# The denominators of a rational convolution: transformed, inverted and scaled in earlier stages

## The reference

```python
a = concat([ones, denumerator])          # 9 taps for each of 64 x 64 channel pairs
b = concat([zeros, numerators])
H_trunc = rfft(b, n=Lx) / rfft(a, n=Lx)  # Lx = 256
H_tf = h0 + rfft(irfft(H_trunc, n=Lx), n=2 * Lx)[0]
Y = einsum('bli,ijl->blj', rfft(x, n=2 * Lx), H_tf)
y = irfft(Y)[..., :Lx, :]
```

## Time and profile before

| | |
|---|---|
| three timed runs | 837.86, 838.05, 841.0 us (median 838.05) |
| the profiled execution | 834.53 us, of which the span of the profile is 832.7 |
| PE busy | 632.0 us (76%) |
| DVE busy | 520.1 us (62%) |
| ACT busy | 330.3 us (40%) |
| POOL busy | 272.7 us (33%) |
| granted TensorE clock, mean | 0.855 of full speed |

### The profile page before, as it was taken

How to read it: one execution, slowest core, us unless ns; L and a number is a source line. 1 busy time by engine, 2 the same in 40 slices (tenths; PEclk the granted TensorE clock), 3 DMA queues, 4 the chain that set the end, 5 groups by cost and what they waited for, 6 DMA issues and landing times. The chain is left out here.

```text
span 832.7 us, 13076 instructions
## 1 busy us (share of the span) xinstructions
PE 632.0 (76%) x4688; PEld 424.1 (51%) x4688; DVE 520.1 (62%) x1402; ACT 330.3 (40%) x634; POOL 272.7 (33%) x233
## 2 busy tenths in 40 slices
PE   3894573776887479999899999977878573998864
PEld 2673462654775342322577878862222122984753
DVE  1242977752655746667457885537466897833897
ACT  1231120443554224455236553223424974931552
POOL 6714701513200101001167674512010798400420
PEclk9995886797999559899899997977888765999987
DMA  7854410100000000000100000040001000000011
GB/s 217 270 176 113 119 39 0 67 3 0 1 1 0 28 41 1 0 2 1 35 6 12 14 7 13 2 179 1 0 1 35 0 1 0 2 3 0 1 26 25
DMA packets 18784, 30.05 MB, mean 36 GB/s; under 512 B 6434, under 2 KB 15650, under 8 KB 18082
## 3 DMA queue, kind: packets, MB, share of 16 engines
q1 hardware_dynamic: 16162, 19.80, 7.8%
q0 software_dynamic: 2560, 9.44, 3.7%
HBM read 27.25 MB, written 1.05 MB: 34 GB/s over the span
## 5 line engine op out<-in xcount | busy, mean ns | idle before, releaser
L166 POOL TENSOR_TENSOR norm_rstd<-norm_var,minus_half 128x16 f32<-128x16 f32 x16 | 46.9, 2929 | 307.8 <-DVE norm_var L160 307.8
L1267 ACT ACTIVATE m_g<-PS,w_slot 128x512 f32<-128x512 f32 x96 | 60.8, 685 | 72.4 <-PE PS L1321 65.0
L1220 DVE TENSOR_TENSOR m_gw<-m_g,PS 128x512 f32<-128x512 f32 x96 | 61.3, 683 | 39.5 <-PE PS L1329 27.3
L1321 PE MATMUL PS<-m_xT,w_slot 64*128 64x512 f32 x192 | 71.7, 698 | 7.0 <-ACT m_g L1267 6.8
L1345 PE MATMUL PS<-m_gw,w_slot 128*64 128x512 f32 x192 | 57.2, 666 | 0.0
L106 PE MATMUL PS<-w_base 128*128 128x128 f32 x316 | 47.4, 307 | 12.5 <-PEq L2647 11.2
L106 PEld LDWEIGHTS PS<-w_base 128*128 128x128 f32 x316 | 41.5, 159 | 15.8 <-issue 13.5
L2066 ACT COPY rat_xf<-PS 64x512 f32<-64x512 f32 x32 | 33.0, 1032 | 9.9 <-PE PS L2122 9.7
L1329 PE MATMUL PS<-m_gT,m_sel 48*128 48x512 bf16 x96 | 24.3, 421 | 15.5 <-DVE m_gw L1220 9.8
L148 DVE BATCH_NORM_STATS2 norm_halves<-H 128x6 f32<-128x64 f32 x256 | 33.8, 209 | 1.2 <-PEq L2647 1.2
L2122 PE MATMUL PS<-w_slot,norm_xn 128*128 128x512 f32 x32 | 24.4, 906 | 13.2 <-DVE norm_xn L2003 13.2
(11 more groups left out here) (339 smaller groups left out, 1634.1 us busy)
## 6 DMA issues: line engine op xcount, KB each, us to landing
rff_routed<-in_routed SPq DMA_DIRECT2D x64, 129.0 KB, 2.1
rat_hf<-in_rat_taps SPq DMA_DIRECT2D x1, 2048.0 KB, 7.8
w_slot<-in_w_rat SPq DMA_DIRECT2D x1, 1589.0 KB, 11.2
w_slot<-in_w_win SPq DMA_DIRECT2D x1, 1378.5 KB, 5.8
w_slot<-in_w_m SPq DMA_DIRECT2D x1, 1329.0 KB, 5.6
w_slot<-in_w_early SPq DMA_DIRECT2D x1, 1092.0 KB, 8.7
out<-H SPq DMA_DIRECT2D x8, 128.0 KB, 2.2
win_v<-win_v SPq DMA_DIRECT2D x8, 97.5 KB, 2.1
```

What stands on the lines that cost most here:

```text
L166: nc.gpsimd.tensor_tensor(N.rstd[:], N.var[:], C.minus_half[:], ALU.pow).then_inc(S["norm_rstd"], 1)
L1220: nc.vector.tensor_tensor(gw[:, i % 2, half, :], g[:, i % 2, half, :], gate_bank[half], ALU.mult)\
L1267: nc.scalar.activation(g[:, i % 2, half, :], hid_bank[(n - 1) % 3], ACT.Gelu, bias=b1[:, s:s + 1])\
L1321: nc.tensor.matmul(hid_bank[n % 3], w1[lane(half), s, :], pair_of(xT, pair)[lane(half)], start=True, stop=True).then_inc(S["hid_ps"], 1)
```

## The change

The numerators' part stays in the rational stage; the denominators' part is distributed over four stages before it. New class `Denominators`:

- `transform(s)` on PE: two matmuls of 32 rows for step s. Steps 0 and 1 stand behind the last chunk of the attention and ahead of batch norm's sums, 2 and 3 behind the sums, 4 and 5 at the end of the stage, 6 and 7 in m1 behind the logits. The transposed results of batch norm use three banks of PSUM in turn, not four.
- `move(s)` on ACT: a copy and a square. Steps 0 to 2 ahead of the rectifiers, 3 to 5 behind them, 6 and 7 in m1 ahead of the exponential, there as four instructions of 128x512 each.
- `add_squares(s)` on DVE: steps 0 to 5 in m1 ahead of the gates, 6 and 7 behind the split. POOL did this before.
- `invert` on DVE: 32 pieces of 128x128 in place of 8 instructions of 128x512: 20 in m1, 8 at the end of win, 4 at the start of m2.
- `scale(s)` on DVE: the denominator times the inverse, 128x1024, 7 between m2's steps and the last behind them. POOL's multiplication of `ht` (L1939) goes.

In the rational stage DVE keeps the products and the norm, POOL keeps an add and a subtract a step, ACT keeps the copies of the token spectra. The taps are loaded in two halves (the denominators' at the start of batch norm's stage), and the small computation at the last frequency (`at_nyquist`) moves from the start to behind the sixth products.

```diff
@@ batchnorm_attention, ACT
             staircase(act, stages, 7)
+            for s in range(SQUARED_FIRST):
+                C.denominators.move(act, s, [PS[2 + s % 2][:]])
             for c in range(CHUNKS):
                 act.wait_ge(S["centred"], c + 1)
                 nc.scalar.activation(junk[:, at], FT[:, at], ACT.Relu, ...).then_inc(S["y"], 1)
+            for s in range(SQUARED_FIRST, SQUARED_TAIL):
+                C.denominators.move(act, s, [PS[2 + s % 2][:]])
@@ batchnorm_attention, PE
+            pe.wait_ge(S["FT"], CHUNKS)
+            denominators(0)
+            denominators(1)
             pe.wait_ge(S["lower_sum"], CHUNKS + 1)
...
+            denominators(2)
+            denominators(3)
             for c in range(CHUNKS):
                 pe.wait_ge(S["y"], c + 1)
-                if c >= W:
-                    pe.wait_ge(S["h_new"], c - W + 1)
+                if c >= 3:
+                    pe.wait_ge(S["h_new"], c - 2)
...
+            for s in range(4, SQUARED_TAIL):
+                denominators(s)
@@ gelu_moe, DVE
+            if again:
+                for s in range(SQUARED_TAIL):
+                    C.denominators.add_squares(v, s)
+            else:
+                for n in range(4 * STEPS - 4, 4 * STEPS - 2):
+                    C.denominators.invert(v, n)
             gate_logits(0)
...
             split_gates(0)
+            if again:
+                for s in range(SQUARED_TAIL, STEPS):
+                    C.denominators.add_squares(v, s)
...
+                if again and i in M1_PIECES:
+                    C.denominators.invert(v, M1_PIECES.index(i))
+                if not again and i in M2_PIECES:
+                    C.denominators.invert(v, 4 * STEPS - 2 + M2_PIECES.index(i))
+                if not again and i in M2_SCALES:
+                    C.denominators.scale(v, M2_SCALES.index(i))
...
+            if not again:
+                C.denominators.scale(v, STEPS - 1)
             add_output(NP - 1)
@@ gelu_moe, ACT: ahead of exponentials(0)
+                for s in range(SQUARED_TAIL, STEPS):
+                    C.denominators.move(act, s, spare_banks[s % 2])
@@ gelu_moe, PE: between logits(0) and hidden(0)
+                for s in range(SQUARED_TAIL, STEPS):
+                    C.denominators.transform(pe, C, s, spare_banks[s % 2])
@@ window_attention, DVE
+                if n in WIN_PIECES:
+                    C.denominators.invert(vec, len(M1_PIECES) + WIN_PIECES.index(n))
@@ new
+SQUARED_FIRST = 3
+SQUARED_TAIL = 6
+M1_PIECES = (1, 3, 4, 5, 6, 7, 8, 9, 13, 16, 17, 19, 21, 23, 24, 25, 27, 28, 29, 30)
+WIN_PIECES = range(580, 644, 8)
+M2_PIECES = (2, 3)
+M2_SCALES = (4, 8, 9, 12, 13, 14, 15)
+    def transform(self, pe, C, s, to):
+        if s >= 2:
+            pe.wait_ge(self.moved, s - 1)
+        for c in range(2):
+            rows = slice(D + c * QUAD, D + (c + 1) * QUAD)
+            self.nc.tensor.matmul(to[c], C["rat_spectrum"][rows, :], self.taps[rows, ...], ...).then_inc(self.made, 1)
+    def move(self, act, s, parts):
+        act.wait_ge(self.made, 2 * s + 2)
+        for j, ps in enumerate(parts):
+            self.nc.scalar.copy(self.of(s)[:, at], ps)
+            ins = self.nc.scalar.activation(self.sq[:, s, at], ps, ACT.Square)
+        ins.then_inc(self.moved, 1)
+    def add_squares(self, v, s):
+        self.nc.vector.tensor_tensor(self.inv[:, s], self.sq[:, s, 0], self.sq[:, s, 1], ALU.add)...
+    def invert(self, v, n):
+        at = self.inv[:, s, k * P:(k + 1) * P]
+        self.nc.vector.reciprocal(at, at).then_inc(self.inverted, 1)
+    def scale(self, v, s):
+        self.nc.vector.tensor_tensor(self.of(s), self.of(s), bcast(self.inv[:, s], 1, 2), ALU.mult)...
@@ rational_convolution, POOL
             def ratio(s):
-                nc.gpsimd.tensor_tensor(ht[...], sums, bcast(inv[:, k], 1, 2), ALU.mult).then_inc(S["ht"], 1)
+                nc.gpsimd.tensor_tensor(to[:, 0], of[:, 0, 0], of[:, 1, 1], ALU.add).then_inc(S["ht"], 1)
+                nc.gpsimd.tensor_tensor(to[:, 1], of[:, 0, 1], of[:, 1, 0], ALU.subtract).then_inc(S["ht"], 1)
@@ rational_convolution, DVE
+            norm_stats(nc, v, S, lambda w: x_of(W + w), N, 1)
             for s in range(STEPS):
                 products(s)
-                if s == 0:
-                    norm_stats(nc, v, S, lambda w: x_of(W + w), N, 1)
-                invert(s)
-                if 2 <= s < 2 + W:
-                    normalise(s + 2)
+                if 1 <= s < 1 + W:
+                    normalise(s + 3)
+                if s == 5:
+                    at_nyquist()
@@ rational_convolution, PE
-                for r in range(4):
+                for c in range(2):
...
+                if g == W - 1:
+                    pe.wait_ge(S["xf"], CHUNKS)
```

187 lines of the change are left out of this document (103 added, 84 removed).

## The result

The changed kernel takes 818.11 us (median of 4 runs, 817.03 to 820.39), the kernel before 838.97 us on the same chip (837.86 to 841.0). The medians are 20.9 us apart; the recorded ratio of the runs, which is not the quotient of these two medians, is 0.9735 with a 95% interval of 0.9713 to 0.9758, which is 22 us (20 to 24). A second set of 6 runs gave 820.09 us and 0.9742 (0.9717 to 0.9767). The forecast was 819.4 us, range 812 to 829.

A forecast was written before the change was run, and what follows sets the result against it. DVE, without slack, sets the rational stage's first part, with POOL's last operation behind it. Terms -29.6 + 2.8 + 3.4 + 1.4 + 2.1 + 1.2 = -18.7 us take 838.05 to 819.4 us, range 812 to 829.

The forecast's parts named there:

- Rational stage, -29.6: Rational stage: DVE loses eight inversions (26.7 us) and waits of 3.6, against 0.3 and 0.4 added; minus 29.6 us.
- the second products wait 0.4 for PE: Rational stage: the second products must wait for PE's second group of matmuls, put at 0.4 us.
- ACT is late by nothing, 0.8 in reserve: Rational stage: ACT, the next bound, is free at 676.8 and first wanted at 677.6, 0.8 us in reserve.
- the rule of the Trainium skill: Rational stage: DVE and POOL exclude each other on SBUF; with POOL less busy, DVE done up to 6.2 us sooner.
- Tail, +2.8: Batch norm's tail: first sum 1.4 us later behind added matmuls, rectifiers another 1.4 behind ACT's square; plus 2.8 us.
- Start of m1, +3.4: Start of m1: the later exponential costs 2.8 us, additions ahead of the expansion 0.6; plus 3.4 us.
- rival A: Tail and start of m1: added matmuls make the clock rise earlier, 5 us more saved, 814.5 us; chance 0.17.
- Steps of m1, +1.4: Steps of m1: PE hides most of the 19.2 us of pieces; those near step 21 cost plus 1.4 us.
- End of win, +2.1: End of win: six pieces ahead of two inverses exceed DVE's idle time there; plus 2.1 us, from 1 to 3.
- m2, +1.2: m2: scalings fall beside PE except step 14's, ahead of the last products; plus 1.2 us, from 0 to 4.
- Rival B: m1 and m2: waits and semaphores expose a third of the pieces, plus 9 us, 828 us; chance 0.15.
- Rivals C and D: C: pieces make PE's clock fall, 850 us, chance 0.04; D: ring waits and dearer places, no change, 838 us, 0.06.

The follow-up runs named there:

- half_ratio: Changed kernel with POOL making only the sum, not the subtraction, in each ratio step of the rational stage: 815.77 us, ratio 0.9714.
- fill_only: Changed kernel without the spread-out denominator work, POOL filling in a constant in m1 instead: 815.14 us, ratio 0.9686.
- best2: Changed kernel with the spread work placed anew, including three inversions in the window stage and seven ahead of m2's logits: 813.86 us, ratio 0.9679.
- after_again: The changed kernel itself, unchanged, run and profiled a second time: 820.09 us, ratio 0.9742.
- m2_slots: Changed kernel with all four m2 inversions ahead of the gate's logits and step 14's scaling moved to step 5: 818.41 us, ratio 0.9722.
- win_three: Changed kernel with three inversions in the window stage instead of eight, the other five ahead of m2's logits: 808.98 us, ratio 0.9696.

## Why the prediction was right, step by step

The time was right, and so was its frame: a large saving in the rational stage against small costs elsewhere. Of the steps some were right. That the sum came so near is in part luck: on the way to m1's logits the clock gave 2.4 us back and in m2 it took 2.0, and the forecast had neither.

- **Rational stage, -29.6:** -28.7 in the profile of the changed kernel. The mechanism was as told: 8 inversions gone, DVE's slack taken up, ACT next. The step "the second products wait 0.4 for PE" failed: it took PE's durations from before, and PE ran the stage's first 6 us at half the clock, so DVE waited 1.96. The step "ACT is late by nothing, 0.8 in reserve" failed for the same reason: its first copy came 5.9 us behind PE's first matmul, not 4.7, and ACT set the end. With the clock at 1.00 POOL does. The four norm pairs took 0.41 + 1.37 us each where 2.51 was taken from before: 2.9 us less, of the 6.2 that the rule of the Trainium skill (SBUF — State Buffer, Who interferes with whom) would have allowed at most. That is not nothing at the end of the stage. POOL follows DVE from step to step, so with the norm of before its last ratio would have ended at about 39.4 us and not at 36.5, and by the two bounds of *half_ratio* the second part's first row would have come at 42.3, not 39.7 (an estimate). The saving on the norm made good DVE's longer wait (1.6 more than forecast) and the small computation at the last frequency, which takes 3.7 us between the products where it took 2.6 at the start.
- **Tail, +2.8:** +2.5, and *fill_only* gives 2.4 back. Both halves are seen: the first sum 1.98 us behind the last `FT` and not 0.89 (+1.1), the rectifiers behind a square (the other 1.4).
- **Start of m1, +3.4:** the chain cost +2.5, DVE waiting 1.6 for the exponential and 1.3 us of additions ahead of the expansion. That the way to the logits would be 2.4 us shorter was not in the forecast, and only in part in rival A. Net +0.1. The four us from 0.23 ahead of the logits, which stood at 0.50, now stand at 0.62, and the four ahead of them at 1.00, where before they had 0.71:

```profile
301.31:305.31 4.00, 2.40 (x20) 2.19 (x20) 0.25 (x1) 1.37 (x2) 0.00 (x0) 1.00 0.01 3
305.31:309.31 4.00, 4.00 (x12) 1.43 (x13) 3.40 (x12) 2.54 (x6) 0.00 (x0) 0.62 0.00 0
```

  This is the largest error, 3.3 us, and its cause stays open: dummies ahead of the barrier do not bring the earlier rise, and *fill_only*, which has neither the transforms nor the later start of m1, loses it.
- **Steps of m1, +1.4:** +1.2 (1.9 against *fill_only*; the four profiles without pieces have 91.7 to 92.5). As forecast, the products of step 25 stand without idle. *best2*, without pieces in steps 21, 23 and 24, is back at 92.34, the number of the kernel before.
- **End of win, +2.1:** +0.7, and +0.2 in *after_again*. The pieces come 0.81 to 0.86 us apart where 0.96 was reckoned, and the inverse behind them takes 0.14, not 0.21. That is about half of the error; the rest stays open.
- **m2, +1.2:** +3.2, where the term was 2.0 too cheap. The scaling of step 14 was right (1.1, given back by *m2_slots*). The other 2.0, of which 1.4 at step 2 and 0.5 ahead of the logits, come from where the clock falls. With five pieces out of the window stage (*win_three*) the delay at step 2 is gone, but only 1.0 to 1.1 us in all; in *best2*, which has other places for the rest too, all of it is.

The terms of the spread work sum to 10.9, the table to 7.7 in one profile and 4.4 in the other, which had the short fall in the window stage; *fill_only* gives back 4.7 in timed runs. The errors had opposite signs: m1's start 3.3 too dear and win 1.4 too dear, m2 2.0 too cheap, and the rational stage's saving 0.9 too large. Rival B, the pieces not hidden, was not seen: the last steps of m1, with a piece in nearly each, run 2.05 to 2.2 us apart, at PE's pace. Rivals C and D were not seen either.

## What to carry to other kernels

Work that is moved into an engine's idle time is free only if nobody waits for a row behind it: here the same operations, in other places, went from 4 to 8 us of cost to none on balance. When an engine's bound is taken away, work out the next one at both levels of the clock, since a stage that starts at half of it can be bound by another engine. And before a delay of one or two us is put down to the instruction ahead of it, look at the same row's duration in a variant without that instruction: in m2's step 2 the row stayed at 1.97 us without its piece.
